# Attention operands stacked in a new row order, loaded onto 32 partitions at a time; values stored as one run per partition

## The reference

```python
# block 1: causal softmax attention, 16 heads of 16
Q = (x @ W_dq @ W_uq);  K = (x @ W_dkv @ W_uk);  V = (x @ W_dkv @ W_uv)
out = softmax(causal(Q K^T / sqrt(16))) @ V;  return out @ W_o
# block 3: phi holds the squares and the scaled pairwise products of 16 features, so phi(q).phi(k) = (q.k)^2 / 16
num = einsum(phi_q, cumsum(phi_k * v));  den = einsum(phi_q, cumsum(phi_k)) + EPS;  return (num / den) @ Wo.T
```

## Time and profile before

| | us |
|---|---|
| median of three runs | 3066.28 |
| profiled execution | 3066.84 |
| its span (first to last instruction) | 3065.1 |
| TensorE matmul busy | 2551.7 (83%) |
| VectorE busy | 2267.6 (74%) |
| ScalarE busy | 1785.7 (58%) |
| GpSimd busy | 542.2 (18%) |
| mean granted TensorE clock | 0.922 of full |

### The profile page before, as it was taken

How to read it: one execution, slowest core, us unless ns; L and a number is a source line. 1 busy time by engine, 2 the same in 40 slices (tenths; PEclk the granted TensorE clock), 3 DMA queues, 4 the chain that set the end, 5 groups by cost and what they waited for, 6 DMA issues and landing times. The chain is left out here.

```text
span 3065.1 us, 60134 instructions
## 1 busy us (share of the span) xinstructions
PE 2551.7 (83%) x15239; PEld 1169.3 (38%) x15239; DVE 2267.6 (74%) x5886; ACT 1785.7 (58%) x2938; POOL 542.2 (18%) x636
## 2 busy tenths in 40 slices
PE   2784989889898998955999997887499999996656
PEld 1441333333333333334566665554122222222545
DVE  5896777778777777646677776999466666665978
ACT  0450566556665666621777774766377777773446
POOL 0341111111111111122000000222222222222300
PEclk9896899989999999978999998999699999998879
DMA  5587464544545445233000000444888888882403
GB/s 163 169 270 165 76 95 70 92 81 81 93 70 93 80 81 92 46 132 108 1 0 0 0 0 28 151 151 158 162 140 139 140 139 137 142 140 83 150 20 109
DMA packets 289396, 309.97 MB, mean 101 GB/s; under 512 B 40496, under 2 KB 243968, under 8 KB 276992
## 3 DMA queue, kind: packets, MB, share of 16 engines
q1 hardware_dynamic: 289280, 308.81, 48.0%
HBM read 181.29 MB, written 126.88 MB: 101 GB/s over the span
## 5 line engine op out<-in xcount | busy, mean ns | idle before, releaser
L818 ACT ACTIVATE a_p<-psum 128x1024 f32<-128x1024 f32 (+3 forms) x768 | 590.0, 814 | 384.2 <-PE psum L921 383.8
L871 DVE CUSTOM_DVE_ANT_0 a_dump<-psum,a_bias 128x256 bf16<-128x256 f32 (+3 forms) x1024 | 451.7, 487 | 175.1 <-PE psum L911 149.0
L911 PE MATMUL psum<-a_ks,a_qs 96*128 96x512 bf16 (+3 forms) x1536 | 469.0, 351 | 131.1 <-DMA a_vs<-values 107.3
L818 ACT ACTIVATE b_p<-psum 128x512 f32<-128x512 f32 (+5 forms) x768 | 453.5, 654 | 167.4 <-PE psum L921 166.5
L921 PE MATMUL psum<-a_qs,a_ks 98*128 98x512 bf16 (+3 forms) x1536 | 395.6, 341 | 5.4 <-ACT a_p L818 3.7
L869 DVE TENSOR_REDUCE a_peak<-psum 128x1 f32<-128x512 f32 x512 | 333.7, 686 | 39.1 <-PE psum L911 37.7
L921 PE MATMUL psum<-b_qs,b_ks 96*128 96x512 bf16 (+3 forms) x1536 | 320.5, 331 | 39.1 <-DMA b_vs<-values 38.8
L935 PE MATMUL psum<-a_p,a_vs 128*32 128x512 f32 (+3 forms) x3072 | 349.3, 529 | 0.6 <-POOL a_p L797 0.4
L845 DVE COPY b_twin<-psum 128x512 f32<-128x512 f32 (+3 forms) x384 | 213.5, 556 | 173.8 <-PE psum L921 172.2
L935 PE MATMUL psum<-b_p,b_vs 128*32 128x512 f32 (+3 forms) x3072 | 328.5, 500 | 8.0 <-POOL b_p L797 8.0
L911 PEld LDWEIGHTS psum<-a_ks,a_qs 96*128 96x128 bf16 x1536 | 135.8, 100 | 495.7 <-issue 155.4
(11 more groups left out here) (187 smaller groups left out, 3263.4 us busy)
## 6 DMA issues: line engine op xcount, KB each, us to landing
qk_parts<-l_parts SPq DMA_DIRECT2D x192, 128.0 KB
a_qs<-qk_parts SPq DMA_DIRECT2D x192, 128.0 KB, 4.7
a_ks<-qk_parts SPq DMA_DIRECT2D x192, 128.0 KB, 7.4
qk_parts<-g_parts SPq DMA_DIRECT2D x192, 128.0 KB, 1.7
b_qs<-qk_parts SPq DMA_DIRECT2D x192, 128.0 KB, 4.7
b_ks<-qk_parts SPq DMA_DIRECT2D x192, 128.0 KB, 8.0
values<-l_vx SPq DMA_DIRECT2D x64, 256.0 KB
a_vs<-values SPq DMA_DIRECT2D x32, 512.0 KB, 9.7
```

The costliest lines, as they stand in the source:

```text
L818: act.activation(p[s % SLOTS][:, 2 * k:2 * k + heads, q0(s):512], m.psum[:, at:at + heads, q0(s):512], ACT.Exp if softmax else ACT.Square, ...
L871: last = dve.tensor_tensor_reduce(dump[c % SRING][:, at:at + w], piece, bias[:, 512 - w:], 1.0, NEG, ALU.add, ALU.max, dst)
L911: last = pe.matmul(m.bank[SB + c % SRING][:, at:at + w], qs[r][0:STACK, hd, qt * P:(qt + 1) * P], ks[r][0:STACK, hd, h * 512:h * 512 + w], ...
```

## The change

- The slots of `qk_dram` are permuted, `Q_SLOT` and `K_SLOT`, so that pairs of parts that are loaded together lie in neighbouring slots.
- `load` goes by halves of the heads (two heads, 4 KB per row). Heads 0 and 1 take rows 0 to 95 in three runs of 32 partitions; heads 2 and 3 take rows 0 to 47 (a run of 16 and one of 32) and 64 to 111 (one of 32 and one of 16), so that rows 48 to 63 hold nothing. In a run of 32 partitions row d of one part and row d of the other stand next to each other, so the rows of one part are two apart. A unit has 14 such transfers for queries and keys and one for the values.
- Rows that no load writes are cleared at the start: four memsets for each ring buffer on VectorE, in both attention passes. The two maxima rows move from 96, 97 to 112, 113; the ones are part of these memsets. Each load and TensorE's first matmul wait for them (`rows_set`).
- Maxima use rows 0 to 111, softmax scores 0 to 113; the second attention uses 96 rows for heads 0 and 1 and 112 for heads 2 and 3.
- The pieces of the maxima alternate between head hd and head hd + 2.
- `v_dram` is [unit, partition, tile, 128], so its load is one run of 4 KB per partition; its stores still write 512 B runs, now 4 KB apart.

```diff
+Q_SLOT = (1, 2, 0)
+K_SLOT = (1, 0, 2)
 STACK = 16 * 6
+MAIN = 16 * 4
+TOP = 16 * 7
...
-        self.v_dram = nc.dram_tensor("values", [z.UNITS, z.S, P], F32, kind="Internal").ap()
+        self.v_dram = nc.dram_tensor("values", [z.UNITS, P, z.ST, P], F32, kind="Internal").ap()
...
-                    at = u * z.GT + t * P
-                    sp.dma_start(m.v_dram[bass.ts(i, z.UPB), at:at + P, :].rearrange("g p k -> p g k"),
+                    sp.dma_start(m.v_dram[bass.ts(i, z.UPB), :, u * G + t, :].rearrange("g p k -> p g k"),
...
-    chunks = [(hd, pieces) for hd in range(HPU) for pieces in (
+    chunks = [(hd, pieces) for hd in range(HPU // 2) for pieces in (
...
-        LOADED = 16 * (2 * STACK // z.DK + 1)
+        LOADED = 16 * 15
...
+        def operand_rows(hd):
+            if softmax:
+                return slice(0, TOP + 2)
+            return slice(0, STACK) if hd < HPU // 2 else slice(0, TOP)
...
             def load(n, r):
-                for tile, which, stack in ((qs[r], 0, Q_STACK), (ks[r], 1, K_STACK)):
-                    row = 0
-                    for first, step, groups in stack:
-                        for part in range(groups):
-                            src = m.qk_dram[first + step * part, which, bass.ts(n, HPU * z.DK), :]
-                            sp.dma_start(tile[row:row + z.DK, :, :].rearrange("p h t -> p (h t)"),
-                                         src.rearrange("(d h) t -> d (h t)", h=HPU)).then_inc(loaded[r], 16)
-                            row += z.DK
-                sp.dma_start(vs[r][:, :, :], m.v_dram[bass.ts(n, 1), :, :].rearrange("n (k p) c -> p (n k) c", p=P)
+                if not isinstance(n, int) or n >= RING:
+                    sp.wait_ge(rows_set, RING)
+                else:
+                    sp.wait_ge(rows_set, n + 1)
+                q, k = [tile[:, :, :].rearrange("p h t -> p (h t)") for tile in (qs[r], ks[r])]
+                parts = [m.qk_dram[:, which, bass.ts(n, HPU * z.DK), :].rearrange("g (d h) t -> d g (h t)", h=HPU)
+                         for which in range(2)]
+                half = z.S * HPU // 2
+                for par, runs in enumerate((((0, 1, 2, 0, 2), (32, 2, 2, 0, 2), (64, 0, 0, 1, 2)),
+                                            ((64, 1, 2, 0, 2), (96, 2, 1, 1, 1), (0, 2, 1, 0, 1), (16, 0, 0, 1, 2)))):
+                    heads = slice(par * half, (par + 1) * half)
+                    for row, q_slot, q_wide, k_slot, groups in runs:
+                        into = slice(row, row + z.DK * groups)
+                        src = parts[0][:, q_slot:q_slot + (1 if q_wide else groups), heads]
+                        if q_wide:
+                            src = src.to_broadcast([z.DK, groups, half])
+                        sp.dma_start(q[into, heads], src).then_inc(loaded[r], 16)
+                        sp.dma_start(k[into, heads], parts[1][:, k_slot:k_slot + groups, heads]
+                                     ).then_inc(loaded[r], 16)
+                sp.dma_start(vs[r][:, :, :], m.v_dram[bass.ts(n, 1), :, :, :].rearrange("n p k c -> p (n k) c")
                              ).then_inc(loaded[r], 16)
...
         def _(dve):
+            for r in range(RING):
+                for tile, fill in ((qs[r], 0.0), (ks[r], 1.0)):
+                    dve.memset(tile[32:MAIN, HPU // 2:HPU, :], 0.0)
+                    last = dve.memset(tile[STACK:P, 0:(HPU if softmax else HPU // 2), :], fill)
+                last.then_inc(rows_set, 1)
...
-            for r in range(RING):
-                last = dve.memset(ks[r][STACK:STACK + 2, :, :], 1.0)
-            last.then_inc(ones_ready, 1)
...
-                    hd, pieces = chunks[c]
+                    hd, pieces = chunks[c // 2][0] + c % 2 * HPU // 2, chunks[c // 2][1]
...
             pe.sem_inc(pv_done, PV)
-            if softmax:
-                pe.wait_ge(ones_ready, 1)
+            pe.wait_ge(rows_set, RING)
...
-                        last = pe.matmul(m.bank[SB + c % SRING][:, at:at + w], qs[r][0:STACK, hd, qt * P:(qt + 1) * P],
-                                         ks[r][0:STACK, hd, h * 512:h * 512 + w], start=True, stop=True)
+                        last = pe.matmul(m.bank[SB + c % SRING][:, at:at + w], qs[r][0:TOP, hd, qt * P:(qt + 1) * P],
+                                         ks[r][0:TOP, hd, h * 512:h * 512 + w], start=True, stop=True)
```

More of the change, by code:

```diff
@@ L40 @@
 PARTS = 3
-Q_STACK = ((0, 0, 3), (1, 0, 2), (2, 0, 1))
-K_STACK = ((0, 1, 3), (0, 1, 2), (0, 1, 1))
+Q_SLOT = (1, 2, 0)
+K_SLOT = (1, 0, 2)
 STACK = 16 * 6
+MAIN = 16 * 4
+TOP = 16 * 7
 class Sizes:
@@ L651, in store_parts @@
         for j in range(4):
-            eng.dma_start(m.qk_dram[part, j // 2, bass.ds(i * z.D + (j % 2) * P, P), u * z.GT:(u + 1) * z.GT],
+            slot = (Q_SLOT, K_SLOT)[j // 2][part]
+            eng.dma_start(m.qk_dram[slot, j // 2, bass.ds(i * z.D + (j % 2) * P, P), u * z.GT:(u + 1) * z.GT],
                           parts[:, part, j, :]).then_inc(stored, 16)
@@ L682, in attend_pass @@
         ((7, 0, 0, 512),), ((7, 1, 0, 512),))]
-    CH = len(chunks)
+    CP = len(chunks)
+    CH = 2 * CP
     assert CH == 3 * STEPS
     SRING = 3
+    EARLY = 9
     with ExitStack() as ctx:
@@ L713, in attend_pass @@
             (bias_zero, bias_ready, peak_set, s_ready, s_taken, npeak_ready, high_ready, split_ready,
-             rows_ready, ones_ready) = sm("bias_zero", "bias_ready", "peak_set", "s_ready", "s_taken", "npeak_ready",
-                                          "high_ready", "split_ready", "rows_ready", "ones_ready")
+             rows_ready) = sm("bias_zero", "bias_ready", "peak_set", "s_ready", "s_taken", "npeak_ready",
+                              "high_ready", "split_ready", "rows_ready")
             ROWS_LOADED = 16 * 8
@@ L719, in attend_pass @@
             twin_ready, d_ready = sm("twin_ready", "d_ready")
+        rows_set, = sm("rows_set")
         block = ctx.enter_context(nc.Block())
+        def operand_rows(hd):
+            if softmax:
+                return slice(0, TOP + 2)
+            return slice(0, STACK) if hd < HPU // 2 else slice(0, TOP)
         def q0(s):
@@ L757, in load_rows @@
                 for k in range(2):
-                    at = qs[r][STACK + k:STACK + k + 1, :, :].rearrange("o h (q b i) -> o (h q) b i", b=4, i=32)
+                    at = qs[r][TOP + k:TOP + k + 1, :, :].rearrange("o h (q b i) -> o (h q) b i", b=4, i=32)
                     for b in range(4):
@@ L862, in maxima @@
             def maxima(n, a, b):
-                for c in range(a, b):
-                    hd, pieces = chunks[c]
+                for c in range(2 * a, 2 * b):
+                    hd, pieces = chunks[c // 2][0] + c % 2 * HPU // 2, chunks[c // 2][1]
                     wait_alone(dve, s_ready, CH * n + c + 1, m.alone)
@@ L889, in unit @@
                 if ahead:
-                    maxima(n + 1, CH // 2, CH)
+                    maxima(n + 1, EARLY, CP)
                     largest(n + 1, (rows_loaded[r], ROWS_LOADED * rnd + ROWS_LOADED))
                 if far:
-                    maxima(n + 2, 0, CH // 2)
-            maxima(0, 0, CH)
+                    maxima(n + 2, 0, EARLY)
+            maxima(0, 0, CP)
             largest(0, None)
-            maxima(1, 0, CH // 2)
+            maxima(1, 0, EARLY)
             all_units(dve, unit)
@@ L920, in scores @@
                 for hd in (2 * k, 2 * k + 1):
-                    last = pe.matmul(m.bank[score_bank(s, hd)][:, q0(s):512], ks[r][0:ROWS, hd, kt * P:(kt + 1) * P],
-                                     qs[r][0:ROWS, hd, h * 512 + q0(s):(h + 1) * 512], start=True, stop=True)
+                    live = operand_rows(hd)
+                    last = pe.matmul(m.bank[score_bank(s, hd)][:, q0(s):512], ks[r][live, hd, kt * P:(kt + 1) * P],
+                                     qs[r][live, hd, h * 512 + q0(s):(h + 1) * 512], start=True, stop=True)
                 last.then_inc(st_ready, 1)
@@ L976, in _ @@
                 pe.wait_ge(loaded[1], LOADED)
-                maximum_scores(1, 1, 0, CH // 2)
+                maximum_scores(1, 1, 0, 2 * EARLY)
             operands(0, 0, 0)
```

## The result

| us | before | after |
|---|---|---|
| median (range) | 3068.57 (3065.55 to 3077.27, 4 runs) | 2983.98 (2982.44 to 2993.09, 4 runs) |
| profiled execution, its span | 3066.84, 3065.1 | 2993.09, 2991.4 |

A forecast was written before the change was run, and what follows sets the result against it. It took operand-load waits and lost clock to bound the first attention pass, TensorE the second. From the profiled 3066.84 us, -111 for waits and +33 for clears gave 2989, 2988 as median; range 2955 to 3040.

The forecast's parts named there:

- What bounds the kernel: First attention pass: TensorE waits 74.2 us in 26 operand loads and its clock drops; second pass: TensorE itself.
- The narrow target: Operand load: 16 partitions hold the rate to 131 GB/s; 32 partitions were taken to give 262.
- The rival by which halves of a pair 8 MB apart cost what the width gains: Operand load gets no faster, stays at 131 GB/s; 3099 us, chance 8%.
- The issue of 14 transfers, 14 x 0.49 = 6.9 us: SP's queue, operand load: 0.49 us per transfer, landing at 11.0 us against a need at 12.4.
- The end that the prediction had worked out: SP's queue: at 0.8 us per three-dimensional issue, 11.2 us in all, and a wait of up to 2.9 us stays.
- -111 us: First attention pass: 19 units without the loop stall save 108 us, the unit ahead of those counted 3.
- Clock: TensorE's granted clock in the first attention pass rises from 0.93 to about 0.97.
- +33 us for the clears: Memsets on VectorE delay the first matmul by 23 us in the first attention pass, 10 in the second.
- At nothing: More matmul rows, values stored as 512 B runs 4 KB apart, and the values' load in 128 runs: each 0.
- A part of the wait stays: Rival, first attention pass: longer issue or about 160 GB/s leaves 1.5 us per unit; 3018 us, chance 15%.
- The clears are cheap: Rival, starts of both attention passes: clears cheap or covered; 2955 to 2970 us, chance 10%.
- VectorE and the rows: Rival, first attention pass: VectorE or the maxima rows become the bound, 1.5 us per unit; 3032 us, chance 12%.

The follow-up runs named there:

- the six transfers: Kernel before with queries and keys loaded in 6 transfers of 256 KB onto 32 partitions, no half heads, no clears, values as before; 2928.9 us, ratio 0.9571.

## Why the prediction was right in time and wrong in two terms

- *What bounds the kernel.* Right: the load wait of attention 1 and the clock lost behind it. In the kernels with no load wait left, or 0.3 us of it, attention 1 takes 905.3 to 916.3 us instead of 1035.5.
- *The narrow target.* Right in kind: 16 partitions read as busy at 131 GB/s, 32 partitions reach 201 to 209 at full share with 8 KB rows. The 262 taken for it was too high. The Trainium skill's ratio, from "SBUF — State Buffer", section "Door 1: The DMA port swizzle" (189 against 104 GB/s), gives an estimated 238 from 131, also more than was measured. The rival by which halves of a pair 8 MB apart cost what the width gains is not borne out: four of the six transfers load such pairs, and the rate was 201 to 209.
- *The issue of 14 transfers, 14 x 0.49 = 6.9 us.* This is the step that failed. It took the price of the old transfers for the new. The three-dimensional ones take 0.56 to 0.63 us recorded and about 0.75 from start to start, the four onto 16 partitions about 0.5, in all 9.65 us. The end that the prediction had worked out (14 x 0.8 = 11.2) was nearer. The rest of the landing, forecast at 1.7 + 2.4 = 4.1, measured 4.16. So 1.4 us to spare became 1.46 us of wait in that unit, 1.7 in the mean of 20.
- *-111 us.* Came out as -81.5 in the profiled executions. The 19 units without the loop stall were to take 26.9 us and took 28.65; their waits of 1.25 to 2.5 us are the difference. Moving the values ahead of the others took the wait away and returned 19 us by the ratios. The nine with the stall took 29.5 us for a forecast of 30.2. The 26.9 itself was right in size and not in its make-up: with six transfers these units take 26.4 and 26.9 us in turn, all of it busy time of TensorE, and no time is lost to the rows, for which 0.3 us had been allowed.
- *Clock.* Forecast 0.97 over the 28 units, measured 0.99. Of the 19 units with a wait 16 stayed at 1.00; the other three, with waits of 1.9 to 2.5 us, were at 0.94. The unit at 601.76 in the earlier trace rows had suggested this; the price of the remaining wait was little more than the wait.
- *+33 us for the clears.* The mis-sized term: +10.8 at the first start and +1.9 at the second, +12.7 together. The ones took 3.74 us start to start (267.97 to 271.71) for a forecast of 4.27; the zeros, 2.01 instead of 4.27 for 4096 elements, made the difference. At the second start TensorE waits for load 0, which lands 12.6 us after its first issue instead of 16.4, and this pays for 3.7 of the 5.6 us by which the clears hold it back; the prediction had it that nothing would cover them. Against the kernel with 12 transfers, the same quick load and no clears, they cost 13.5 + 4.7 = 18 us.
- *At nothing.* Rows and order: 0 within the intervals. Values' stores: the first memset behind the latent pass starts at 262.78 us, at 263.13 before, so that pass did not grow. Values' load: counted at 0, worth 15 us while there was a wait.
- *Rivals.* "A part of the wait stays" is what happened, by the mechanism it names; it would have been 3018 with the clears at +33. "The clears are cheap" happened as well, in part. The gain fell short by 29.5 us, the clears cost 20.3 less than forecast, and the stretch between the attention passes happened to be 4.1 shorter; with under 1 us more in the rest, 4.3 us are left. That the time came out is luck, the mechanism is not. VectorE and the rows did not become the bound (one row wait of 2.2 us).

## What to carry to other kernels

When a transfer is made quicker by a better shape, work out again what feeds it: price the issue by instructions of the new shape, start to start, and compare bytes per issue with the engines' rate; a DMA share of half with a queue full of issues means fewer and larger transfers. Put the transfer with the longest landing first in a group that one wait covers. A forecast that hits may hide errors that cancel: compare it term by term.

## What the runs showed of the hardware that was not expected

- A three-dimensional DMA occupied SP's queue for about 0.75 us within units whether it moved 64, 128 or 256 KB, a two-dimensional one 0.49 us; 88, 175 and about 205 GB/s followed. At the start of a pass, with TensorE still idle, the three-dimensional ones were 0.63 us apart at all three sizes (275.35 to 275.98 us in after). No run shows what makes the difference.
- A memset that the program writes over bf16 zeros ran as uint32: 2048 elements of it (8 KB) in 1.76 us, where 4096 bf16 ones took 3.47.
- While transfers with two parts outermost ran, 0.12 to 0.13 of the 16 engines were busy, that is 2, at 45 to 53 GB/s.
- TensorE's load waits of 1.25 to 2.5 us left the granted clock of 16 of 19 units of after at 1.00; the wait of 3.78 us in the earlier trace rows had been followed by 0.50 (1.2 GHz).
